# Ordering 100,000 edges on one core: sources ranked by block of 128 nodes with one product per 16 columns and a scan, both ends' counts and weight sums in one product

## The reference

```python
deg_out = segment_sum(edge_weight, src); deg_in = segment_sum(edge_weight, dst)
norm = edge_weight * rsqrt(deg_out[src] * deg_in[dst] + EPS)
h = relu(segment_sum((h @ W)[src] * norm[:, None], dst) + b)      # layer 0, twice
ns = segment_sum(mid(y[dst], edge MLP), src); deg = segment_sum(1, src)   # layer 1
out = segment_sum(h_src * softmax_over_dst(alpha), dst)           # layer 2, attention
msg = segment_sum(scaled[dst], src); dinv = rsqrt(1 + segment_sum(1, dst))  # layer 3
```

## Time and profile before

| | us |
|---|---|
| median of 3 runs | 10853.75 (10845.99 to 10910.27) |
| the profiled execution | 10899.97 |
| its span, first to last instruction | 10898.1 |
| busy in the span: TensorE, VectorE, ScalarE, POOL | 6667.6, 6021.7, 2957.7, 5779.3 |

### The profile page before, as it was taken

The page is one execution under the profiler, slowest core; times in us unless marked ns, Lnnn a source line. Parts: engine busy times, 40 slices in busy tenths (PEclk is TensorE's granted clock), DMA queues, the critical chain, the costliest instruction groups (busy, mean ns, idle before and its releaser), DMA issues. The chain is left out here.

```text
span 10898.1 us, 113673 instructions
## 1 busy us (share of the span) xinstructions
PE 6667.6 (61%) x25911; PEld 3879.9 (36%) x25911; DVE 6021.7 (55%) x19329; ACT 2957.7 (27%) x9449; POOL 5779.3 (53%) x6086
## 2 busy tenths in 40 slices
PE   3544445555884545566666777774556668956665
PEld 2443334443443333433334111143333333333332
DVE  8555544443004776644444999966555579943333
ACT  1000010102873222200001877751222226600000
POOL 2566566665003767566661888842555530036665
PEclk8666666556997676766666999986666669966655
DMA  3111111111555333333332555542666645523334
GB/s 100 44 44 48 40 46 50 46 46 50 179 173 155 95 94 94 84 92 92 92 92 72 175 172 171 172 100 76 186 191 184 195 129 176 175 71 93 92 93 83
DMA packets 790810, 1188.79 MB, mean 109 GB/s; under 512 B 162029, under 2 KB 633523, under 8 KB 777229
## 3 DMA queue, kind: packets, MB, share of 16 engines
q0 software_dynamic: 246400, 552.44, 19.5%
q1 hardware_dynamic: 543757, 629.10, 17.6%
HBM read 923.59 MB, written 257.40 MB: 108 GB/s over the span
## 5 line engine op out<-in xcount | busy, mean ns | idle before, releaser
L1071 POOL DMA_INDIRECT ring<-scaled_table,idx_s x832 | 787.1, 946 | 1167.1 <-DVEq L188 774.5
L951 POOL DMA_INDIRECT big<-x_table,rec_d_sb x808 | 815.2, 1009 | 1068.4 <-DMA x_table<-big 720.3
L1652 POOL DMA_INDIRECT ring<-att_table,rec_d_sb x808 | 775.4, 960 | 820.2 <-DVE acc L1764 296.7
L1323 PE MATMUL bank<-ring,wts 128*128 128x512 f32 x1664 | 931.1, 643 | 377.1 <-issue 134.0
L307 POOL DMA_INDIRECT rec_s<-acc,big x784 | 791.7, 1010 | 685.4 <-DVE big L532 435.4
L1997 PE MATMUL bank<-ring 128*128 128x256 f32 x1664 | 787.4, 618 | 415.3 <-DVE ring L1979 227.7
L1245 POOL DMA_INDIRECT ring<-y_table,idx_s x832 | 814.2, 979 | 401.5 <-DVEq L188 190.9
L1098 PE MATMUL bank<-ring 128*128 128x256 f32 x1616 | 753.4, 594 | 418.5 <-issue 395.8
L307 POOL DMA_INDIRECT rec_d<-x_res,big x784 | 798.2, 1018 | 394.0 <-issue 251.1
L1071 POOL DMA_INDIRECT ring<-h_table,rec_d_sb x808 | 765.7, 948 | 450.2 <-PE bank L1098 212.0
L1033 PE MATMUL bank<-big,ring 128*128 128x256 f32 x1616 | 611.8, 553 | 595.8 <-issue 464.7
(11 more groups left out here) (316 smaller groups left out, 13831.9 us busy)
## 6 DMA issues: line engine op xcount, KB each, us to landing
weights_dram<-acc SPq DMA_DIRECT2D x104, 1024.0 KB, 4.5
ring<-weights_dram SPq DMA_DIRECT2D x832, 128.0 KB
rows_spill<-ring SPq DMA_DIRECT2D x808, 128.0 KB
big<-rows_spill SPq DMA_DIRECT2D x808, 128.0 KB, 2.2
ring<-key_dram SPq DMA_DIRECT2D x98, 1024.0 KB
big<-dl_dram SPq DMA_DIRECT2D x50, 512.0 KB
ring<-y_table,idx_s POOLq DMA_INDIRECT x832
ring<-scaled_table,idx_s POOLq DMA_INDIRECT x832
```

Of the source, the lines that this page charges most:

```text
L951: g.indirect_dma_start(out=xg[:, c % RG, :], out_offset=None, in_=x_table, in_offset=bass.IndirectOffsetOnAxis(ap=recd3i[:, c, D_IDX:D_IDX ...
L1071: g.indirect_dma_start(out=slot[:, c % ring_len, :], out_offset=None, in_=table, in_offset=bass.IndirectOffsetOnAxis(ap=index(c), axis=0)) ...
L1323: pe.matmul(ps[6 + u % 2], oh1[c // 4 % 2][:, c % 4, :], mid[:, c % 2, 0:512], start=(c % GS == 0), stop=(c % GS == GS - 1)).then_inc(summ ...
L1652: g.indirect_dma_start(out=ag[:, n % R3, :], out_offset=None, in_=att_table, in_offset=bass.IndirectOffsetOnAxis(ap=recd3i[:, n, D_IDX:D_I ...
```

## The change

The sources are no longer ranked by node but by block: within a block of 128 nodes the edges stand by column and lane, which is enough for sums by one-hot of the lane. It takes two passes over block one-hots of 400 elements, laid out block by column. The first (blocks_vector, blocks_tensor) counts the edges of each block with one matmul a batch. The second adds two matmuls a batch (places_tensor: all lanes' sum of each column, and minus the lanes at or behind one's own), and block_places_vector runs a scan along the columns of each block (restart, zero at each block's first column, starts it anew), adds the block's running start (base), selects by the one-hot and reduces. No transposes, picks, spread keys or compares are needed, and ScalarE has no part in it.

Both ends are then counted in 98 batches: the right operand of the 16 matmuls is the block one-hot times four columns (1 and three parts of the weight, cnt_w, 128x1600), so counts and weight sums come out of one product of width 100. L428 and L501 go. The destinations are ranked as before. POOL waits for each quarter of the attributes when it comes to it, and for the fields of each table apart, and the fields of the destinations' table are staged behind the sources' rows. Only the destinations' keys are turned, written and spread. (key_dram, hot buffers and banks are laid out anew; table_rows is the unchanged second half of rows_vector; unit_starts that of start_vector.)

```diff
@@ -297,11 +308,12 @@
             g.iota(number_d, [[1, JD]], base=0, channel_multiplier=JD,
                    allow_small_or_imprecise_dtypes=True).then_inc(number_made.s, 1)
             g.wait_ge(prefilled.s, 32)
-            g.wait_ge(attrs_staged.s, 4 * QUARTERS)
-            g.wait_ge(fields_staged.s, 1)
             for k, (stage, table, landed) in enumerate(((stage_s, rec_s_dram, scattered_s),
                                                         (stage_d, rec_d_dram, scattered_d))):
+                g.wait_ge(fields_staged.s, k + 1)
                 for j in range(EJ):
+                    if k == 0 and j % EH == 0:
+                        g.wait_ge(attrs_staged.s, 4 * (j // EH + 1))
                     if j % BJ == 0:
                         g.wait_ge(rows_ready.s, k * NBATCH + j // BJ + 1)
                     g.indirect_dma_start(
...
-            sp.wait_ge(key_out.s, 64)
-            for k in range(2):
-                for b in range(NBATCH):
-                    at_b = k * NBATCH + b
-                    if at_b >= 2:
-                        sp.wait_ge(bcast_used.s, at_b - 1)
-                    sp.dma_start(bcast[at_b % 2].rearrange("p j e -> p (j e)"),
-                                 key_dram[k][b * BJ:(b + 1) * BJ].rearrange("(o j) p -> o (j p)", o=1)
-                                 .to_broadcast([P, BJ * P])).then_inc(bcast_in.s(at_b, 2), 16)
+            sp.wait_ge(key_kept.s, 1)
+            sp.dma_start(key_dram[0:6 * P].rearrange("(g j) p -> j g p", g=6),
+                         turned_key[:, 0:6 * P].rearrange("j (g p) -> j g p", g=6)).then_inc(key_out.s, 16)
+            sp.dma_start(key_dram[6 * P:EJ], turned_key[0:EJ - 6 * P, 6 * P:7 * P]).then_inc(key_out.s, 16)
+            sp.wait_ge(key_out.s, 32)
+            for b in range(NBATCH):
+                if b >= 2:
+                    sp.wait_ge(bcast_used.s, bcast_used.n(b - 1))
+                sp.dma_start(bcast[b % 2].rearrange("p j e -> p (j e)"),
+                             key_dram[b * BJ:(b + 1) * BJ].rearrange("(o j) p -> o (j p)", o=1)
+                             .to_broadcast([P, BJ * P])).then_inc(bcast_in.s(b, 2), 16)
...
+
+        def blocks_tensor():
+
+            for b in range(NBATCH):
+                pe.wait_ge(blocks_hot.s, b + 1)
+                pe.matmul(ps[0][:, 0:BJ * NB], ones_b, hot_b[b % 2],
+                          start=(b == 0), stop=(b == NBATCH - 1)).then_inc(blocks_counted.s, 1)
+
+        def places_tensor(b):
+
+            pe.wait_ge(blocks_hot.s, NBATCH + b + 1)
+            if b >= 2:
+                pe.wait_ge(rows_ready.s, b - 1)
+            pe.matmul(ps[2 + b % 2][:, 0:BJ * NB], ones_b, hot_b[b % 2], start=True, stop=True)
+            pe.matmul(ps[4 + 3 * (b % 2)][:, 0:BJ * NB], at_or_behind, hot_b[b % 2],
+                      start=True, stop=True).then_inc(blocks_summed.s, 1)
 
         def count_tensor(k, b):
 
             at_b = k * NBATCH + b
             pe.wait_ge(counted_hot.s, at_b + 1)
             for q in range(BJ):
-                ins = pe.matmul(ps[0][:, k * NB:(k + 1) * NB], cnt_lo[at_b % 2][:, q, :], cnt_hi[at_b % 2][:, q, :],
+                ins = pe.matmul(counts[k], cnt_lo[at_b % 2][:, q, :],
+                                cnt_w[at_b % 2][:, q].rearrange("p s k -> p (s k)"),
                                 start=(b == 0 and q == 0), stop=(b == NBATCH - 1 and q == BJ - 1))
             ins.then_inc(counted_used.s, 1)
...
-            for q in range(BJ):
-                pe.matmul(ps[6][:, k * P:k * P + 3 * NB], hot_lo[at_b % 2][:, q, :],
-                          hot_w[at_b % 2][:, q].rearrange("p s k -> p (s k)"),
-                          start=(b == 0 and q == 0), stop=(b == NBATCH - 1 and q == BJ - 1))
-
-        def pick_tensor(k, b):
-
-            at_b = k * NBATCH + b
-            pe.wait_ge(prefix_kept.s, at_b + 1)
-            if at_b >= 1:
-                pe.wait_ge(rows_ready.s, at_b)
...
         def prepare_tensor():
+            pe.wait_ge(consts.s, 2)
+            blocks_tensor()
+            pe.wait_ge(keys_ready.s, 1)
+            for q in range(7):
+                width = min(P, EJ - q * P)
+                ins = pe.transpose(key_bank[q // 4][0:width, (q % 4) * P:(q % 4 + 1) * P],
+                                   key_f[:, q * P:q * P + width], ident)
+            ins.then_inc(key_turned.s, 1)
+            for b in range(NBATCH):
+                places_tensor(b)
+            pe.wait_ge(key_kept.s, 1)
             for k in range(2):
-                pe.wait_ge(keys_ready.s, k + 1)
-                for q in range(7):
-                    width = min(P, EJ - q * P)
-                    ins = pe.transpose(key_bank[k][q // 4][0:width, (q % 4) * P:(q % 4 + 1) * P],
-                                       key_f[k][:, q * P:q * P + width], ident)
-                ins.then_inc(key_turned.s, 1)
+                for b in range(NBATCH):
+                    count_tensor(k, b)
+            start_tensor()
+            pe.wait_ge(rows_ready.s, NBATCH)
             for b in range(NBATCH):
-                count_tensor(0, b)
-            start_tensor(0)
-            pe.wait_ge(key_kept.s, 2)
-            for b in range(NBATCH):
-                rank_tensor(0, b)
-                count_tensor(1, b)
-                pick_tensor(0, b)
-            start_tensor(1)
-            for b in range(NBATCH):
-                rank_tensor(1, b)
-                pick_tensor(1, b)
+                rank_tensor(b)
+                pick_tensor(b)
...
+        def blocks_vector(b, pass_i):
+            at_b = pass_i * NBATCH + b
+            if pass_i == 0:
+                if b >= 2:
+                    v.wait_ge(blocks_counted.s, b - 1)
+            elif b >= 2:
+                v.wait_ge(blocks_summed.s, b - 1)
+            v.tensor_tensor(hot_b[b % 2].rearrange("p (k j) -> p k j", k=NB), lanes(iota_p[:, 0:NB], NB, BJ),
+                            rows(key_hi[0][:, b * BJ:(b + 1) * BJ], NB, BJ), ALU.is_equal).then_inc(blocks_hot.s, 1)
+
+        def block_starts_vector():
+            v.wait_ge(blocks_counted.s, NBATCH)
+            then_v(v.tensor_reduce(units, ps[0][:, 0:BJ * NB].rearrange("p (k j) -> p k j", k=NB), AX.X, ALU.add))
+            unit_starts(GS * P, units, ends_s)
+            then_v(v.tensor_scalar(base, firsts, float(GS * P), None, ALU.mult))
+
+        def block_places_vector(b):
+
+            js = slice(b * BJ, (b + 1) * BJ)
+            v.wait_ge(blocks_summed.s, b + 1)
+            then_v(v.tensor_tensor_scan(behind, restart, ps[2 + b % 2][:, 0:BJ * NB], 0.0, ALU.mult, ALU.add))
+            then_v(v.tensor_tensor(behind3, behind3, lanes(base, NB, BJ), ALU.add))
+            v.tensor_copy(base, behind3[:, :, BJ - 1])
+            then_v(v.tensor_tensor(sums, behind, ps[4 + 3 * (b % 2)][:, 0:BJ * NB], ALU.add))
+            then_v(v.tensor_tensor(sums, sums, hot_b[b % 2], ALU.mult))
+            then_v(v.tensor_reduce(place, sums.rearrange("p (k j) -> p j k", k=NB), AX.X, ALU.add))
+            table_rows(0, js, b, NCS)
 
         def count_vector(k, b):
             js, at_b = slice(b * BJ, (b + 1) * BJ), k * NBATCH + b
             if at_b >= 2:
                 v.wait_ge(counted_used.s, at_b - 1)
             v.tensor_tensor(cnt_lo[at_b % 2], rows(iota_p, BJ, P), lanes(key_lo[k][:, js], BJ, P), ALU.is_equal)
-            v.tensor_tensor(cnt_hi[at_b % 2], rows(iota_p[:, 0:NB], BJ, NB), lanes(key_hi[k][:, js], BJ, NB),
-                            ALU.is_equal).then_inc(counted_hot.s, 1)
-
-        def start_vector(k, unit, ends):
-
-            v.wait_ge(counted_used.s, (k + 1) * NBATCH)
-            if k:
-                v.wait_ge(prefix_done.s, NBATCH)
-            then_v(v.tensor_copy(nodes, ps[0][:, k * NB:(k + 1) * NB]))
-            v.drain().then_inc(totals.s, 1)
-            v.wait_ge(offsets_in.s, k + 1)
-            then_v(v.tensor_scalar(units_i, ps[0][:, 5 * NB:6 * NB], float(unit - 1), None, ALU.add))
+            then_v(v.tensor_tensor(hot_hi[at_b % 2], rows(iota_p[:, 0:NB], BJ, NB), lanes(key_hi[k][:, js], BJ, NB),
+                                   ALU.is_equal))
+            v.tensor_tensor(cnt_w[at_b % 2], hot_hi[at_b % 2].rearrange("p j (o k) -> p j o k", o=1)
+                            .to_broadcast([P, BJ, 4, NB]),
+                            w_part[:, :, js].rearrange("p s (j o) -> p j s o", o=1).to_broadcast([P, BJ, 4, NB]),
+                            ALU.mult).then_inc(counted_hot.s, 1)
+
+        def degrees_vector(k, deg):
+            v.tensor_copy(deg[:, NB:2 * NB], counts[k][:, 0:NB])
+            then_v(v.tensor_reduce(deg[:, 0:NB], counts[k][:, NB:4 * NB].rearrange("p (s b) -> p b s", s=3),
+                                   AX.X, ALU.add))
+
...
+        def start_vector():
+
+            then_v(v.tensor_copy(nodes, deg_d_first[:, NB:2 * NB]))
+            v.drain().then_inc(totals.s, 1)
+            v.wait_ge(offsets_in.s, 1)
+            unit_starts(P, ps[0][:, 5 * NB:6 * NB], ends_d)
```

(85 more changed lines are left out.)

167 lines of the change are left out of this document (71 added, 96 removed).

## The result

The changed kernel takes 11,135.5 us (median of 4 runs, 11,095.5 to 11,164.6) against 10,855.2 (4 runs): a ratio of 1.0245, 95% interval 1.0219 to 1.0272. It is slower, where I forecast 10,820 us. The profiled execution has a span of 11,144.9 us, 246.8 more than before.

What follows compares the result with a forecast made beforehand. POOL's unbroken scatters, holding up TensorE, were taken to pace the ranking stages. Preparation was to end at 1434 + 1170 = 2604 us against 2642.7 (−39); 10853.75 − 35 gave about 10,820 us, range 10,590 to 10,950.

Steps and rivals of the forecast that it cites:

- The second pass: Placing the sources within blocks: 5.05 us a batch on VectorE, 254 us with padding, ending near 300 us.
- the free 130: Ranking stages: some 130 matmuls issue freely after POOL restarts; a pause of about 7 us gives them back.
- hold-up: Preparation before the edge MLP: TensorE barely moves while POOL scatters without a break, 1.33 to 2.45 us a matmul.
- The slower rival: Starved second pass: VectorE waits for TensorE's sums, POOL runs dry; +252 us, 11,106 us, chance 0.11.
- My condition against it: Against the starved pass: slow stretches start at the same number of matmuls, not at the same time.
- Scatter of the sources: POOL's 784 source scatters: from near 50 us, 989 us plus some 25 for lengthened ones, ending near 1064 us.
- Counting: Both ends, 98 batches: 4.68 us each alone, 39 under scatters; 21 done by 1064 us, ending at 1428.
- Ranking the destinations: Last stage before the edge MLP: starts at 1434 us, paced by POOL, takes 1170 us, ends at 2604.
- the cycle of three batches with a long pause: Destinations' ranking: POOL pauses about 14 us every three batches, 74.6 us a cycle, 1220 us in all.
- first pass: Block counting replacing source counting: 49 one-hots with a matmul each, 29 us, from about 8 to 37 us.
- the return of the early scatter's gain: Counting behind the source scatter: 77 batches, 360 us, stand alone, mostly giving back the gain of scattering early.
- The rule on fetching instructions: Trainium skill, against the hold-up: instructions stream by each engine's own queue, so issue is no limit; some 9,660 us.

Runs made afterwards that it cites:

- the four extra copies: Changed kernel with four more 16-element copies per batch of the second pass, waited for or not: 11,188.8 and 11,155.2 us, ratios 1.021 and 1.018.
- the pass with POOL silent: Changed kernel with POOL's source scatters held back until all 49 batches of rows are made: 11,037.8 us, 1.002 of the kernel before.

## Why the prediction was wrong

- *The second pass* is the step whose mechanism failed: "TensorE has two matmuls a batch, 98 in all, under the free 130, so I expect no hold-up here; at 2.45 us each they would still be 4.9 us, no longer than VectorE's 5.05". I had found the hold-up on TensorE and priced it in matmuls. It is charged to VectorE's instructions as well, and the pass has 13: 13 x 2 x 0.70 = 18.2 us, not 5.05. Shown by the grid, by the four extra copies and by the pass with POOL silent. The pass took 886 us instead of 254. The sum of the pieces that I forecast for VectorE was right (5.2 us until 76 us).
- *In size* the part of the destinations failed as much. Of the 268 us between the forecast end of the part (2604) and the measured one (2872), 58 are the longer scatter of the sources, 79 the counting behind it and 131 the ranking of the destinations.
- *The slower rival* had the outcome (11,106 us, +252; measured 11,135, +280) by luck and not by its road: there was no wait for sums, and POOL never ran dry. That the counting comes behind the scatters (92 of 98 batches) is what happened. My condition against it (slow stretches start at a number of matmuls) was read from stages in which matmuls were most of the instructions.
- *Scatter of the sources*: from 51 us as forecast, to 1122 instead of 1064. It made six stops of 3 us, one every 113 scatters, and had lengthened scatters throughout (mean distance 1.36 us in the second pass, not 1.262).
- *Counting*: 44.8 us a batch under the scatters (forecast 39), 4.54 alone (4.68). It began at 952 instead of 314 us, so 6 batches were done instead of 21 (58 us more behind the scatters), and after the last scatter 25 us passed before VectorE went on, not 4 (21 us more). It ended at 1565 instead of 1428.
- *Ranking the destinations*: the cycle of three batches with a long pause, which I had only as an upper bound of 1220 us, was the case, and it took some 80 us instead of 74.6: 1302 us in all, where I took 1170. I had counted the product's going as a gain of 45 us (shorter scatters) and matmuls as what lengthens the cycle; the runs show that it is the product's going that does. Its start took 5 us (6 forecast).
- *Right*: first pass (by 36 us), the first scatter, VectorE at 99% alone with POOL idle, the MLP's own length (673 us, 677 before), the return of the early scatter's gain, though more than all of it went. What comes behind the MLP took 23 us more than before in the profiled executions, 0.3% of it.
- *The rule on fetching instructions* that I weighed against the hold-up was beside the point: in the counting 16 matmuls go in 1.52 us and only their signal is late, so the hold-up lies behind the instructions, not in their fetching. "The trace disagrees" was said too soon.

## What to carry to other kernels

When an engine stands idle beside a queue that runs without a break, ask for the shape of the waits in every engine's timeline, one that waits only for itself above all: equal steps point to a common toll, and here what pays it is the number of instructions, not their work. An overlap can then cost more than it hides, and a small pause in the stream that does the crowding can be worth more than any saving beside it. Here 0.36 us behind each scatter turned a change that lost 2.5% into one that wins 5.8% (one run) and, with the pauses placed, 8.7%. Most of that is the pauses' and not the change's: the old kernel with its own pauses wins 6.2%. Try the pause on both kernels before you credit the change.

## What the runs showed of the hardware

- Under indirect scatters 1.26 us apart at the median (1.35 to 1.37 on average in the slow stretches), each instruction of VectorE costs two steps of 0.70 us (second pass) and each matmul with its weight load four (counting, MLP); with a scatter every 1.62 us none. Records per scatter (64 or 128) play no part.
- It doesn't begin at once: some 130 matmuls in the earlier trace rows, four steps each, are about 520, if a backlog has to fill first. The Trainium skill ("NOTIFIC — the notification-queue block", section "The implicit engine gate") has a profile record the start and the end of every instruction, and (section "Constraints, capacities, measured rates") some 500 records in flight in the block. Two steps an instruction agree with the first, and 520 with the second. But the second pass speaks against one size of backlog: there the slow steps began when, since POOL's first scatter, VectorE had issued 60 instructions and all engines together 104, which makes 208 steps. And if the steps are these records, then that a record costs the engine zero cycles, in the same section, does not agree with 0.70 us a step. That they are is argued, not shown. All runs here were recorded in the same way, so whether the hold-up, and the gain of the pauses, exist without recording is open.
- Dense bf16 products of VectorE lengthen scatters, from 0.96 to 1.71 us beside one of 1600 elements (94 of 94 in one stage), and the same counting ran free where it met POOL's scatters near their start (4.54 us a batch) and slow where it came behind 860 us of slow steps (44.8). That these are two stable states of one system, and that the lengthened scatters hold it in the free one, is argued; at a scatter every 1.36 us the second pass went slow and free again by itself.
